# Summing the constant row b2 Wv Wo on VectorE from the PSUM blocks of Wv Wo, in place of 24 TensorE passes

## The chip, the core and the metric

The kernel runs on one core of a Trainium2 chip: TensorE (PE) with its weight loads (PEld), VectorE (DVE), ScalarE (ACT), GpSimd (POOL), and SyncE (SP), which issues most DMAs. The metric is the device time of one execution in microseconds (us), inputs and output in HBM. Lower is better.

## What is computed

Sixteen batches of 256 rows of 512 go through one cross-attention over a context of 384 columns and then a feed-forward layer with ternary weights. The part that matters here is the attention's value path:

```python
x2 = layernorm(modality2, ln2_g, ln2_b)      # (.. - mu) * rsqrt(var + EPS) * g2 + b2
v  = x2 @ Wv + bv
attn = softmax(q @ k.T * scaling)
ctx = attn @ v
return ctx @ Wo + bo
```

The rows of `attn` sum to one, so what does not depend on the row of the context leaves the softmax unchanged. With n the normalised context without gain and bias, the result is attn n diag(g2) Wv Wo plus one constant row, (b2 Wv + bv) Wo + bo. The kernel prepares the matrix diag(g2) Wv Wo (`Wvo`, three blocks of 128 rows by 512) and the constant row (`crow`, repeated over all 128 partitions) once, in its prologue.

## The kernel before

Eight groups of 512 rows (two batches, four tiles of 128 rows) are worked on. The body of group b does the feed-forward layer of b (16 steps of `up`, `sq`, `hi`, `lo`, `down`) and, between them, the attention of group b+1. All of it runs in float32, or in pairs of a high half (ScalarE writes it) and a low half (VectorE writes it by subtraction).

Before the first body there is a prologue of about 95 us. It prepares the weights and does the attention of group 0. It is written out by hand: one list of words for each engine (`PROLOGUE`, L166 on), and each engine works through its list in order. Engines meet by semaphores only. The words that matter here:

- `turn:n` (PE), `sides:n` or `tern:n` (DVE), `abs:n` and `store:n` (ACT): the 32 pieces of the ternary weights. ACT sums absolute values of a piece (L817), POOL makes scales from four sums (`scale`, L633 to L640), DVE compares (`sides`: L1093, L1094; `tern`: L1088, L1089), PE turns the piece into an O bank (L1339, L1343), ACT stores it (L837). `sides:n` and `tern:n` wait for `turn:n-4`; `turn:n` waits for `store:n-4`.
- Jobs, in the order of PE's list (`JOBS`). Job n writes bank H0 or H1, whichever n's parity says, and first waits until the bank's last reader is done with job n-2 (`job_read`). For a job that both ACT and DVE read, that is DVE's semaphore `job_dve`.
- `wvT:c`: transpose of a block of Wv, copied by ACT (L687). `wvo:c`: block c of Wv Wo, eight passes from `WvT` and `Wo_s` (L1167). ACT writes the high half scaled by g2 (L695), then DVE the low half (L892).
- `bv:0`: b2 Wv as a column, 24 passes of `Wv_s` against b2 (L1152); DVE adds bv and writes `bvp` (L882). `coacc` (DVE): the four blocks of Wo, each scaled by a column of `bvp`, summed into `bvrep` (L1034, L1036), each of the four waiting for the one before. `co:0`: PE sums `bvrep` over the partitions with a matrix of ones (L1171), DVE adds bo and writes `crow` (L897).
- `M:c`: blocks of Wq Wk^T (L1160, low half L887). `n1T:t`, `n2T:t`: transposes of the normalised input tiles (L1209); ACT makes those inputs (`nx`, L767; `nc`, L793). `fb:0` (L1176): the low-rank part. `t:0` to `t:2` (L1183): the first products of group 0's attention; they need M and all transposes.

At the prologue's end ACT normalises group 1's rows (L767), and SyncE issues their moves as small DMAs (L505), on which group 1's `t` waits in body 0.

Of the kernel before, what the change touches and what calls it, by code (L numbers as in the profile page):

```python
# [29 lines left out]
P = 128  # L30
ALU = mybir.AluOpType
# [5 lines left out]
HI, LO = 0, 1  # L37
# [109 lines left out]
def body_steps(b, engine):  # L147
# [11 lines left out]
    for j in (NFF - 3, NFF - 2):  # L159
# [62 lines left out]

JOB_KINDS = ("wqT", "wkT", "M", "bq", "wvT", "bv", "wvo", "co", "fb")
JOBS = [(word.partition(":")[0], int(word.partition(":")[2])) for word in PROLOGUE["pe"]
# [3 lines left out]
def mk_xattn_ffn(nc, x, ctx_768, ln1_g, ln1_b, ln2_g, ln2_b, Wq, bq, Wk, bk, Wv, bv, Wo, bo,  # L228
# [7 lines left out]
    NG = NB * S // TOK  # L236
# [7 lines left out]
    with ExitStack() as stack:  # L244
# [22 lines left out]
        bvc = vcols[:, 2 * KD + 2 * KC:NV]  # L267
        bvp = sb("bvp", [P, KE])
        gatec = sb("gatec", [P, 1])
# [105 lines left out]
        ident_made, identb_made, ones_made = sem("ident_made"), sem("identb_made"), sem("ones_made")  # L375
        bq_summed, co_summed = sem("b1_Wq_summed"), sem("bv_Wo_summed")
        tb_products, tb_made = sem("tbias_products"), sem("tbias_made")
# [100 lines left out]
        def _(sp):  # L478
# [79 lines left out]
            for b in range(NG - 1):  # L558
# [12 lines left out]
                if b + 2 < NG:  # L571
                    move_n1(b + 2)
            store(6, 0)
            for t in range(3):
# [271 lines left out]
        def _(dve):  # L846
# [14 lines left out]
            def job(n):  # L861
# [15 lines left out]
                elif kind == "bq":  # L877
                    dve.wait_ge(bq_in, 16)
                    nc.vector.tensor_tensor(x2a[:, KC, :], bank[:, :], bqrow, ALU.add).then_inc(job_dve, 1)
                elif kind == "bv":  # L880
                    dve.wait_ge(vcols_made, 1)
                    nc.vector.tensor_tensor(bvp[:, :], bank[:, :].rearrange("p (k n) -> p k n", k=KE)[:, :, 0], bvc[:, :],  # L882
                                            ALU.add).then_inc(job_dve, 1)
                    dve.wait_ge(job_dve, job_count(n, "dve"))
                elif kind == "M":
# [4 lines left out]
                elif kind == "wvo":  # L890
                    dve.wait_ge(job_act, job_count(n, "act"))
                    nc.vector.scalar_tensor_tensor(out=Wvo[:, LO, c, :], in0=bank[:, :], scalar=g2c[:, c:c + 1],  # L892
                                                   in1=Wvo[:, HI, c, :], op0=ALU.mult, op1=ALU.subtract
                                                   ).then_inc(job_dve, 1)
                elif kind == "co":
# [71 lines left out]
            def steps(b, todo, odd=None):  # L967
# [3 lines left out]
                for st in todo:  # L971
# [58 lines left out]
                    elif kind == "coacc":  # L1030

                        acc = bvrep[:, :, :].rearrange("p k n -> p (k n)")
                        dve.wait_ge(wo_in, 16)
                        link(nc.vector.tensor_scalar(acc, Wo_s[:, 0, :], bvp[:, 0:1], None, ALU.mult))  # L1034
                        for k in range(1, KE):
                            last = nc.vector.scalar_tensor_tensor(out=acc, in0=Wo_s[:, k, :], scalar=bvp[:, k:k + 1],  # L1036
                                                                  in1=acc, op0=ALU.mult, op1=ALU.add)
                            if k < KE - 1:
                                link(last)
                        last.then_inc(co_summed, 1)  # L1040
                    elif kind[:2] in ("xs", "cs"):
# [83 lines left out]
        def _(pe):  # L1125
            pe.wait_ge(ident_made, 1)

            def job(n):
# [14 lines left out]
                elif kind == "bq":  # L1143
# [3 lines left out]
                    mm = pe.matmul(bank[:, :], ones[:, :], x2a[:, 0, :], start=True, stop=True)  # L1147
                elif kind == "bv":
                    pe.wait_ge(vcols_made, 1)
                    for e in range(KE):  # L1150
                        for k in range(KC):
                            mm = pe.matmul(bank[:, e * P:(e + 1) * P], Wv_s[:, k, e * P:(e + 1) * P],  # L1152
                                           b2c[:, k:k + 1].broadcast_to([P, P]), start=(k == 0), stop=(k == KC - 1))
                elif kind == "M":
# [14 lines left out]
                elif kind == "co":  # L1169
                    pe.wait_ge(co_summed, 1)  # L1170
                    mm = pe.matmul(bank[:, :], ones[:, :], bvrep[:, :, :].rearrange("p k n -> p (k n)"),  # L1171
                                   start=True, stop=True)
                elif kind == "fb":
                    pe.wait_ge(lowrank_in, 16 * 7)
                    for k in range(KD):
                        mm = pe.matmul(bank[:, k * 64:(k + 1) * 64], v_s[:, k * P:(k + 1) * P],  # L1176
                                       fbT4[:, :, :].rearrange("s i r -> s (i r)"), start=True, stop=True)
# [226 lines left out]
```

## Time and profile before

| | |
|---|---|
| median of 3 runs | 805.66 us (803.67 to 807.49) |
| the profiled execution's own time | 805.04 us |
| its span in the trace | 803.0 us |
| PE busy in the span | 777.0 us (97%), 3877 matmul instructions |
| PEld busy | 642.9 us (80%) |
| DVE busy | 543.3 us (68%) |
| ACT busy | 374.9 us (47%) |
| POOL busy | 150.0 us (19%) |

The span runs from the first to the last instruction seen, and 2.04 us of the execution lie around it. The shares are means over the whole span; the change lies in some 25 us of the prologue, whose shares are others. A row of the timeline gives start and length; rows of one engine overlap a little, because the length runs to the end of writing. So what an instruction costs its engine is read from its start to the next one's.

### The profile page before, as it was taken

What the parts mean: (1) busy time and instruction counts of PE and PEld (TensorE: products, weight loads), DVE (VectorE), ACT (ScalarE), POOL (GpSimd) and SP (SyncE); (2) the same over time, 40 slices, a digit from 0 to 9 for tenths busy, and PEclk for the clock granted to TensorE, in tenths of its full rate; (3) what the DMA queues carried; (4) which work ended last, traced back from release to release, by engine and by line L of the source; (5) the groups of instructions that cost most, each with busy time, mean ns of one, the idle gap of its engine ahead of it and who ended that gap; (6) DMA issues with size and microseconds to landing.
All of it is one profiled execution on the core that took longest, in us unless ns stands there. A gap on an engine that the chain in (4) does not pass through costs nothing.

```text
span 803.0 us, 10829 instructions
## 1 busy us (share of the span) xinstructions
PE 777.0 (97%) x3877; PEld 642.9 (80%) x3877; DVE 543.3 (68%) x1100; ACT 374.9 (47%) x705; POOL 150.0 (19%) x171
## 2 busy tenths in 40 slices
PE   6999988999999999999999999999999999999998
PEld 4678767887888778887888788887888788888886
DVE  5998857667757685577766685577766686476434
ACT  5997545335551644326542554326542554424332
POOL 3241130112202022022201122012301122012001
PEclk9999999999999999999999999999999999999999
DMA  9753141034410551134410452124420441021001
GB/s 314 273 144 102 17 77 56 36 54 69 127 40 1 85 112 53 40 46 69 118 57 1 70 86 94 40 36 74 98 83 0 70 75 55 0 35 45 27 0 53
DMA packets 180554, 56.93 MB, mean 71 GB/s; under 512 B 167666, under 2 KB 168068, under 8 KB 180500
## 3 DMA queue, kind: packets, MB, share of 16 engines
q1 hardware_dynamic: 150368, 51.51, 26.2%
q10 hardware_dynamic: 30132, 4.73, 3.4%
q8 instruction: 31, 0.51, 0.3%
q14 instruction: 23, 0.19, 0.1%
HBM read 27.64 MB, written 8.39 MB: 45 GB/s over the span
## 4 chain that ended last, share of the span: by engine, by line
PE 77%; SPq 6%; DVE 5%; ACT 3%; ACTq 3%; DMA 3%; issue 2%; DVEq 0%
PE G L1183 23%; PE O L1299 22%; PE H L1318 22%; SPq L505 5%; ACTq L788 3%; PE H L1324 3%; DVE rbuf L1074 2%; DMA Wv_s<-in_L_xattn_Wv_dram 2%; ACT rbuf L749 1%; PE H L1167 1%; PE G L1265 1%; PE O L1372 1%; DMA n_blocks<-n_rows 1%; PE H L1183 1%; ACT qbuf L757 1%
## 5 line engine op out<-in xcount | busy, mean ns | idle before, releaser
L1299 PE MATMUL O<-projT,qbuf 128*128 128x512 f32 x992 | 246.9, 391 | 6.7 <-DVE qbuf L1078 6.7
L1299 PEld LDWEIGHTS O<-projT,qbuf 128*128 128x128 f32 x992 | 184.1, 188 | 47.7 <-DVE qbuf L1078 10.6
L757 ACT ACTIVATE qbuf<-rbuf 128x512 fp32r<-128x512 f32 x125 | 79.1, 633 | 148.5 <-DVE rbuf L1074 112.1
L1074 DVE TENSOR_TENSOR rbuf<-rbuf 128x512 f32<-128x512 f32 x128 | 95.5, 746 | 61.9 <-ACT rbuf L749 61.8
L1318 PE MATMUL H<-even_group,fcT 128*128 128x512 f32 x512 | 127.8, 392 | 2.9 <-ACT rbuf L749 2.9
L1318 PE MATMUL H<-odd_group,fcT 128*128 128x512 f32 x512 | 127.3, 391 | 0.0
L749 ACT ACTIVATE rbuf<-H,scf 128x512 f32<-128x512 f32 x128 | 86.9, 679 | 68.2 <-PE H L1324 63.2
L1318 PEld LDWEIGHTS H<-even_group,fcT 128*128 128x128 f32 x512 | 94.9, 188 | 22.4 <-ACT rbuf L749 3.3
L1078 DVE TENSOR_TENSOR qbuf<-rbuf,qbuf 128x512 fp32r<-128x512 f32 x125 | 88.8, 710 | 33.7 <-ACT qbuf L757 30.9
L1318 PEld LDWEIGHTS H<-odd_group,fcT 128*128 128x128 f32 x512 | 95.3, 188 | 19.3
L1183 PE MATMUL G<-Wvo,tT 128*128 128x512 f32 x270 | 65.6, 391 | 0.0
L1183 PEld LDWEIGHTS G<-Wvo,tT 128*128 128x128 f32 x270 | 50.5, 188 | 11.2 <-DVE tT L944 0.4
L1324 PE MATMUL H<-tstack,uT 128*128 128x512 f32 x128 | 49.9, 390 | 0.0
L617 POOL TENSOR_TENSOR nrs<-nrs,mhalf 128x1 f32<-128x1 f32 x32 | 25.7, 804 | 125.3 <-DVE nrs L924 125.3
L612 POOL TENSOR_TENSOR xrs<-xrs,mhalf 128x4 f32<-128x4 f32 x8 | 8.4, 1051 | 187.7 <-DVE xrs L1058 187.7
L940 DVE SCALAR_TENSOR_TENSOR tT<-G,tbias,tT 128x512 fp32r<-128x512 f32 x23 | 17.2, 748 | 30.8 <-ACT tT L730 30.8
L767 ACT ACTIVATE n_rows<-xb,xnm,xrs 128x512 f32<-128x512 f32 x28 | 22.4, 811 | 29.9 <-issue 29.9
L1183 PE MATMUL G<-odd_group,M 128*128 128x512 f32 x144 | 33.6, 390 | 2.2 <-DVE tT L940 2.2
L1183 PEld LDWEIGHTS G<-n2T,tT 128*128 128x128 f32 x261 | 33.6, 190 | 2.5 <-DVE tT L940 1.4
L1183 PE MATMUL G<-n2T,tT 128*128 128x256 f32 x261 | 35.0, 283 | 0.0
L944 DVE TENSOR_TENSOR tT<-G,tT 128x512 fp32r<-128x512 f32 x22 | 15.2, 691 | 27.6 <-ACT tT L733 27.6
L1183 PEld LDWEIGHTS G<-odd_group,M 128*128 128x128 f32 x144 | 27.0, 188 | 8.1 <-DVE tT L940 2.6
(196 smaller groups left out, 1066.9 us busy)
## 6 DMA issues: line engine op xcount, KB each, us to landing
xb<-in_x_dram SPq DMA_DIRECT2D x8, 1024.0 KB, 4.8
n_blocks<-n_rows SPq DMA_DIRECT2D x112, 64.0 KB, 2.3
ctxb<-in_ctx_dram SPq DMA_DIRECT2D x8, 768.0 KB, 4.3
n_blocks<-ctxb SPq DMA_DIRECT2D x112, 48.0 KB, 2.1
wring<-in_L_ffn_w_fc_dram SPq DMA_DIRECT2D x16, 256.0 KB, 5.3
wring<-in_L_ffn_w_proj_dram SPq DMA_DIRECT2D x16, 256.0 KB, 3.1
out_dram<-x2a SPq DMA_DIRECT2D x8, 512.0 KB, 3.0
x_blocks<-x_rows SPq DMA_DIRECT2D x56, 64.0 KB, 3.0
```

Of the source, the lines that this page charges most:

```text
L505: sp.dma_start(*block_of(blocks, rows, i, q)).then_inc(moved, 16)
L617: nc.gpsimd.tensor_tensor(nrs[:, t:t + 1], nrs[:, t:t + 1], mhalf[:, 0:1], ALU.pow).then_inc(rstd_made, 1)
L749: nc.scalar.activation(rbuf[:, j % 2, :], banks[f"H{j % 2}"][:, :], ACT.Relu, scale=scf[:, j:j + 1]).then_inc(relu_made, 1)
L757: nc.scalar.activation(squares(b, j)[:, HI, :], rbuf[:, j % 2, :], ACT.Copy).then_inc(sqhi_made, 1)
L767: nc.scalar.activation(nrm[:, t % 2, :] if g == 0 else n1_rows[:, t, :], xb[:, t, :], ACT.Identity, scale=xrs[:, t:t + 1], bias=xnm[:, t:t ...
L788: act.dma_start(*block_of(x_blocks, x_rows, i, q)).then_inc(x_moved, 16)
L1074: nc.vector.tensor_tensor(rbuf[:, j % 2, :], rbuf[:, j % 2, :], rbuf[:, j % 2, :], ALU.mult).then_inc(square_made, 1)
L1078: nc.vector.tensor_tensor(squares(b, j)[:, LO, :], rbuf[:, j % 2, :], squares(b, j)[:, HI, :], ALU.subtract).then_inc(sqlo_made, 1)
L1183: mm = pe.matmul(bank, w, m, start=(first and i == 0), stop=(last and i == len(pairs) - 1))
L1299: mm = pe.matmul(banks[f"O{t}"][:, :], qbuf[:, j % 2, h, t * P:(t + 1) * P], projT[:, j, :], start=(j == 0 and h == HI), stop=(j == NFF - ...
L1318: pe.matmul(banks[f"H{j % 2}"][:, :], fcT[:, k, j * P:(j + 1) * P], xnT[:, h, k, :], start=(k == 0 and h == HI), stop=False)
L1324: pe.matmul(banks[f"H{j % 2}"][:, :], uT[:, j * P:(j + 1) * P], tstack[:, :], start=False, stop=True).then_inc(up_full, 1)
```

## The change

The job `bv:0` goes, with its 24 passes, `bvp` and its addition. `coacc` now scales Wo's blocks by bv alone and stands ahead of `wvo:0` in DVE's list. Each `wvo:c` on DVE gets a second instruction: after the low half it adds b2's column times the block as it stands in PSUM (before the gain) to the same `bvrep`. `co:0` waits for the last of these. Since b2 Wv Wo is the sum over all rows of Wv Wo scaled by b2, and `co:0` sums over partitions, `crow` comes out the same.

```diff
     "pe": (
...
-        "n1T:1 M:2 turn:4 turn:5 bv:0 turn:6 turn:7 wvT:2 n1T:2 wvo:0 turn:8 turn:9 n1T:3 turn:10 turn:11 wvo:1 wvo:2 "
+        "n1T:1 M:2 turn:4 turn:5 turn:6 turn:7 wvT:2 n1T:2 wvo:0 turn:8 turn:9 n1T:3 turn:10 turn:11 wvo:1 wvo:2 "
...
     "dve": (
...
-        "sides:6 tern:7 cs23 n1T:0 n1T:1 M:2 bv:0 tern:8 tern:9 tern:10 sides:11 sides:12 tern:13 wvo:0 sides:14 "
-        "tern:15 coacc n1T:2 n1T:3 wvo:1 wvo:2 tern:16 sides:17 sides:18 co:0 sides:19 n2T:0 n2T:1 M:3 n2T:2 n2T:3 "
+        "sides:6 tern:7 cs23 n1T:0 n1T:1 M:2 tern:8 tern:9 tern:10 sides:11 sides:12 tern:13 coacc wvo:0 sides:14 "
+        "tern:15 n1T:2 n1T:3 wvo:1 wvo:2 tern:16 sides:17 sides:18 co:0 sides:19 n2T:0 n2T:1 M:3 n2T:2 n2T:3 "
...
-JOB_KINDS = ("wqT", "wkT", "M", "bq", "wvT", "bv", "wvo", "co", "fb")
+JOB_KINDS = ("wqT", "wkT", "M", "bq", "wvT", "wvo", "co", "fb")
...
                 elif kind == "wvo":
                     dve.wait_ge(job_act, job_count(n, "act"))
                     nc.vector.scalar_tensor_tensor(out=Wvo[:, LO, c, :], in0=bank[:, :], scalar=g2c[:, c:c + 1],
-                                                   in1=Wvo[:, HI, c, :], op0=ALU.mult, op1=ALU.subtract
-                                                   ).then_inc(job_dve, 1)
+                                                   in1=Wvo[:, HI, c, :], op0=ALU.mult, op1=ALU.subtract)
+                    acc = bvrep[:, :, :].rearrange("p k n -> p (k n)")
+                    dve.wait_ge(co_parts, KE)
+                    if c > 0:
+                        dve.wait_ge(job_dve, job_count(JOBS.index(("wvo", c - 1)), "dve"))
+                    nc.vector.scalar_tensor_tensor(out=acc, in0=bank[:, :], scalar=b2c[:, c:c + 1], in1=acc,
+                                                   op0=ALU.mult, op1=ALU.add).then_inc(job_dve, 1)
...
                         dve.wait_ge(wo_in, 16)
-                        link(nc.vector.tensor_scalar(acc, Wo_s[:, 0, :], bvp[:, 0:1], None, ALU.mult))
+                        dve.wait_ge(vcols_made, 1)
+                        nc.vector.tensor_scalar(acc, Wo_s[:, 0, :], bvc[:, 0:1], None, ALU.mult).then_inc(co_parts, 1)
                         for k in range(1, KE):
-                            last = nc.vector.scalar_tensor_tensor(out=acc, in0=Wo_s[:, k, :], scalar=bvp[:, k:k + 1],
-                                                                  in1=acc, op0=ALU.mult, op1=ALU.add)
-                            if k < KE - 1:
-                                link(last)
-                        last.then_inc(co_summed, 1)
+                            dve.wait_ge(co_parts, k)
+                            nc.vector.scalar_tensor_tensor(out=acc, in0=Wo_s[:, k, :], scalar=bvc[:, k:k + 1],
+                                                           in1=acc, op0=ALU.mult, op1=ALU.add).then_inc(co_parts, 1)
...
                 elif kind == "co":
-                    pe.wait_ge(co_summed, 1)
+                    job_read(pe, JOBS.index(("wvo", KC - 1)))
```

VectorE's instructions from block 0 of `Wvo` to its block 1 (`wvo:0`, `sides:14`, `tern:15`, `coacc`, the n1 halves, `wvo:1` and `wvo:2`) stand so before:

```order
L892 SCALAR_TENSOR_TENSOR Wvo<-H,vcols,Wvo 128x512 [waits job_act,job_full]
L1093 TENSOR_SCALAR above<-wring,half 128x512 [waits tern_turned,scales_made]
L1094 TENSOR_SCALAR below<-wring,minus_half 128x512
L1088 TENSOR_SCALAR below<-wring,minus_half 128x512 [waits tern_turned,scales_made]
L1089 SCALAR_TENSOR_TENSOR above<-wring,half,below 128x512 [waits dve_chain]
L1034 TENSOR_SCALAR bvrep<-x2a,bvp 128x512 [waits wo_in]
L1036 SCALAR_TENSOR_TENSOR bvrep<-x2a,bvp,bvrep 128x512 [waits dve_chain] x3
L934 TENSOR_TENSOR even_group<-G,even_group 128x4x128 [waits unit_act] x2
L892 SCALAR_TENSOR_TENSOR Wvo<-H,vcols,Wvo 128x512 [waits job_act,job_full] x2
```

The same place on VectorE in the changed program (its line numbers are its own; `x2a` is the buffer that holds Wo):

```order
L1034 TENSOR_SCALAR bvrep<-x2a,vcols 128x512 [waits vector_columns_made,wo_in]
L1037 SCALAR_TENSOR_TENSOR bvrep<-x2a,vcols,bvrep 128x512 [waits bv_Wo_parts_summed] x3
L886 SCALAR_TENSOR_TENSOR Wvo<-H,vcols,Wvo 128x512 [waits job_act,job_full]
L892 SCALAR_TENSOR_TENSOR bvrep<-H,vcols,bvrep 128x512 [waits bv_Wo_parts_summed]
L1091 TENSOR_SCALAR above<-wring,half 128x512 [waits tern_turned,scales_made]
L1092 TENSOR_SCALAR below<-wring,minus_half 128x512
L1086 TENSOR_SCALAR below<-wring,minus_half 128x512 [waits tern_turned,scales_made]
L1087 SCALAR_TENSOR_TENSOR above<-wring,half,below 128x512 [waits dve_chain]
L933 TENSOR_TENSOR even_group<-G,even_group 128x4x128 [waits unit_act] x2
L886 SCALAR_TENSOR_TENSOR Wvo<-H,vcols,Wvo 128x512 [waits job_act,job_full]
L892 SCALAR_TENSOR_TENSOR bvrep<-H,vcols,bvrep 128x512 [waits job_dve,bv_Wo_parts_summed]
```

The four instructions of `coacc` moved from behind `tern:15` to ahead of block 0's low half, and each block now has two instructions that read its bank (the third pair follows).

TensorE's passes for the three blocks, the ones product (`co`) and the last block of M, with the banks' numbers, before:

```order
L1167 MATMUL H1<-x2a,WvT 128x512 [waits job_act,wo_in,job_dve]
...
L1167 MATMUL H0<-x2a,WvT 128x512 [waits job_act]
...
L1167 MATMUL H1<-x2a,WvT 128x512 [waits job_act,job_dve]
...
L1171 MATMUL H0<-bvrep,ones 128x512 [waits bv_Wo_summed,job_dve]
L1160 MATMUL H1<-WkT,WqT 128x384 [waits job_act,job_dve]
```

The same in the changed program:

```order
L1159 MATMUL H0<-x2a,WvT 128x512 [waits job_act,wo_in,job_dve]
...
L1159 MATMUL H1<-x2a,WvT 128x512 [waits job_act]
...
L1159 MATMUL H0<-x2a,WvT 128x512 [waits job_act,job_dve]
...
L1163 MATMUL H1<-bvrep,ones 128x512 [waits job_dve]
L1152 MATMUL H0<-WkT,WqT 128x384 [waits job_act,job_dve]
```

With one job less the banks change places; the third block still waits for VectorE to have read the first, and the ones product now waits for VectorE's last reading of the third block.

## Rows read from the trace of the kernel before

**Rows 1.** Busy time by stretch: length, each engine busy (count), clock, DMA share.

```profile
31.00:46.00 15.00, 15.00 (x94) 9.05 (x93) 13.73 (x26) 14.56 (x35) 3.50 (x10) 1.00 0.61 170
46.00:54.00 8.00, 8.00 (x63) 6.02 (x62) 7.62 (x18) 7.95 (x22) 4.18 (x7) 1.00 0.40 134
...
124.00:803.00 679.00, 668.36 (x3194) 558.90 (x3194) 447.78 (x886) 288.39 (x512) 114.65 (x107) 1.00 0.26 55
```

**Rows 2.** The chain that ended last, prologue: start, length, what.

```profile
28.52 2.73 PE H L1152 x24
...
32.81 3.44 PE H L1167 x8
36.24 0.45 PE O L1339 x8
...
37.80 6.92 PE H L1167 x16
...
53.62 2.98 PE G L1183 x12
```

**Rows 3.** The same chain, from the prologue's end into body 0.

```profile
92.57 2.94 ACT n_rows L767 x4
95.53 0.75 SPq L505
...
123.95 3.02 PE G L1183 x12
```

**Rows 4.** Timeline of VectorE: start, length, what, idle before it and releaser.

```profile
30.25 0.61 DVE L887 SCALAR_TENSOR_TENSOR M<-H,vcols,M 128x384 fp32r<-128x384 f32 x1
31.29 0.16 DVE L882 TENSOR_TENSOR bvp<-H,vcols 128x4 f32<-128x4 f32 x1 [0.44 <-PE H L1152]
31.49 0.49 DVE L1088 TENSOR_SCALAR below<-wring,minus_half 128x512 bf16<-128x512 f32 x1
...
36.58 0.49 DVE L1093 TENSOR_SCALAR above<-wring,half 128x512 bf16<-128x512 f32 x1 [0.65 <-PE O L1339]
...
37.37 0.48 DVE L1088 TENSOR_SCALAR below<-wring,minus_half 128x512 bf16<-128x512 f32 x1
...
38.56 0.75 DVE L892 SCALAR_TENSOR_TENSOR Wvo<-H,vcols,Wvo 128x512 fp32r<-128x512 f32 x1
39.22 0.48 DVE L1093 TENSOR_SCALAR above<-wring,half 128x512 bf16<-128x512 f32 x1
...
41.20 0.48 DVE L1034 TENSOR_SCALAR bvrep<-x2a,bvp 128x512 f32<-128x512 f32 x1
41.71 2.33 DVE L1036 SCALAR_TENSOR_TENSOR bvrep<-x2a,bvp,bvrep 128x512 f32<-128x512 f32 x3
43.95 1.28 DVE L934 TENSOR_TENSOR even_group<-G,even_group 128x512 fp32r<-128x512 f32 x2
45.15 1.41 DVE L892 SCALAR_TENSOR_TENSOR Wvo<-H,vcols,Wvo 128x512 fp32r<-128x512 f32 x2
46.47 0.48 DVE L1088 TENSOR_SCALAR below<-wring,minus_half 128x512 bf16<-128x512 f32 x1
```

**Rows 5.** Timeline of GpSimd.

```profile
31.15 0.22 POOL L640 TENSOR_SCALAR minus_half<-scf 128x4 f32<-128x4 f32 x1
```

**Rows 6.** Timeline of ScalarE.

```profile
34.66 0.85 ACT L767 ACTIVATE nrm<-xb,xnm,xrs 128x512 f32<-128x512 f32 x1
35.37 1.11 ACT L837 ACTIVATE fcT<-O 128x512 fp32r<-128x512 f32 x2
...
44.76 0.69 ACT L695 ACTIVATE Wvo<-H,vcols 128x512 fp32r<-128x512 f32 x1 [0.24 <-PE H L1167]
```

**Rows 7.** Timeline of TensorE: three places.

```profile
9.38 1.97 PE L1142 MATMUL H<-ident,Wq_s 128*128 128x128 f32 x8 [3.03 <-ACT WqT L684]
...
46.24 1.08 PE L1171 MATMUL H<-bvrep,ones 128*128 128x512 f32 x2
...
89.98 0.63 PE L1209 MATMUL H<-ident,nrm 128*128 128x128 f32 x4 [1.26 <-DVE nrm L1067]
```

More of the change, by code:

```diff
@@ L267, in mk_xattn_ffn @@
         bvc = vcols[:, 2 * KD + 2 * KC:NV]
-        bvp = sb("bvp", [P, KE])
         gatec = sb("gatec", [P, 1])
@@ L375, in mk_xattn_ffn @@
         ident_made, identb_made, ones_made = sem("ident_made"), sem("identb_made"), sem("ones_made")
-        bq_summed, co_summed = sem("b1_Wq_summed"), sem("bv_Wo_summed")
+        bq_summed, co_parts = sem("b1_Wq_summed"), sem("bv_Wo_parts_summed")
         tb_products, tb_made = sem("tbias_products"), sem("tbias_made")
@@ L572, in _ @@
                     move_n1(b + 2)
-            store(6, 0)
+            store(NG - 2, 0)
             for t in range(3):
@@ L879, in job @@
                     nc.vector.tensor_tensor(x2a[:, KC, :], bank[:, :], bqrow, ALU.add).then_inc(job_dve, 1)
[L880 to L884, printed above, removed]
                 elif kind == "M":
@@ L1147, in job @@
                     mm = pe.matmul(bank[:, :], ones[:, :], x2a[:, 0, :], start=True, stop=True)
[L1148 to L1153, printed above, removed]
                 elif kind == "M":
```

## The prediction

> **What bounds the kernel now.** I read first the busy time by stretch, for the stretch that the change touches, since the shares of the whole span say nothing of it. TensorE is busy 15.00 of 15.00 us from 31 to 46 us, but VectorE is at 13.73 and ScalarE at 14.56; from 46 to 54 us it is 8.00 of 8.00 with VectorE at 7.62 and ScalarE at 7.95 [rows 1]. Three engines are full at once, so work can't be passed from one to another for free. The chain of waits comes second. It stays on TensorE through the prologue's middle: the 24 passes with b2 (2.73 us), the block 0 of Wv Wo (3.44 us), blocks 1 and 2 (6.92 us), and so on to the product `t:0` at 53.62 us [rows 2]. Seen from this chain alone, 24 passes less are 2.73 us less. The third view is the timeline of each engine around the same places; it tells who would be late once the passes are gone. Last, what a shift at `t:0` does later: the chain goes on over ScalarE's n rows at 92.57 us, the queue of SyncE that moves them from 95.53 us, and arrives at group 1's `t:0` at 123.95 us [rows 3]. Each of these waits for the one before and none for a fixed moment; in the bodies TensorE is busy 668.36 of 679.00 us [rows 1]. So a shift of `t:0` in the prologue reaches the end one to one.
>
> **The prices.** A step costs from its start to the next one's start.
> - `tern` costs 1.19 us (37.37 to 38.56) and `sides` 0.79 (36.58 to 37.37) [rows 4].
> - The low half of a block costs VectorE 0.66 us (38.56 to 39.22; two in 1.32, 45.15 to 46.47), with its data in PSUM. The new instruction has the same form, operands and size, so 0.66 as well. Bounds: nothing below 0.66, and 0.75 if it waits for its predecessor, as in `coacc`, where three took 2.24 us from 41.71 to 43.95 [rows 4]. I take 0.66: between two additions into `bvrep` stands a low half.
> - `coacc` costs 2.75 us (41.20 to 43.95), the two halves of n1T 1.20 (43.95 to 45.15) [rows 4]. It is moved, not changed: still four instructions, each waiting for the one before.
> - Removed on VectorE: `bvp` with 0.20 us (31.29 to 31.49), and 0.44 us of waiting for TensorE ahead of it [rows 4].
>
> The Trainium skill ("VectorE: DVE Perf Modes", section "The DRAIN you can't avoid") says that a semaphore after each VectorE operation costs nothing extra. The rows disagree by a little: 0.75 with such a wait and 0.66 without it. By the page `coacc` would take some 0.3 us less, and my estimate would come out near +1.3 us and not +1.6; the sum goes by the rows.
>
> **TensorE, until it must wait.** Without the passes it reaches `turn:6` 2.73 us earlier, and then meets other waits.
> 1. Block 0 (`wvo:0`) is now job 14 and needs job 12, `M:2`, read by VectorE: that row runs from 30.25 to 30.86 [rows 4]. So it starts at 30.95 at the earliest and ends at 34.4 (3.44 us), 1.8 us earlier than before.
> 2. `n1T:3` needs ScalarE's row that runs from 34.66 to 35.51, and `turn:11` needs the second of the two stores from 35.37 to 36.48 [rows 6]. ScalarE is full and doesn't wait for TensorE there, so neither comes earlier. Then 0.45 us of turning [rows 2], and block 1 starts at 37.0. Before, it started 0.7 us later. Of the 2.73 us, 2.0 are lost by here.
> 3. Block 1 ends at 40.4. Block 2 needs block 0 read by VectorE, now by both instructions.
>
> **VectorE.** `tern:8` started at 31.49, behind `bvp`. But it needs GpSimd's scales too, and the last of those ends at 31.37 [rows 5], so it starts at about 31.45: the 0.44 us of waiting stay. The wait of 0.65 us ahead of `sides:12` [rows 4] is for `turn:8`, which now ends at 34.6, and goes. From 31.45: three `tern` (35.0), two `sides` (36.6), `tern:13` (37.8), `coacc` (40.55), low half and addition of block 0, 2 x 0.66 (41.9). Before, the low half of block 0 was read at 39.3. `coacc` ahead of it, 2.75 us, is on TensorE's path now: what is queued behind it is the reading that frees block 2's bank.
>
> **The stall.** Block 2 starts on TensorE at 42.0, when it could at 40.4: a new wait of 1.5 us. It ends at 45.5, where before blocks 1 and 2 together ended at 44.7. ScalarE's high half of block 2, at 44.76 before with 0.24 us of waiting [rows 6], comes at 45.7 and ends at 46.35. VectorE, from 41.9: `sides:14` (42.7), `tern:15` (43.9), n1T (45.1), block 1's pair (46.4), block 2's pair (47.7, written at 47.85). Both routes arrive together at 46.4.
>
> **The ones product** started at 46.24 [rows 7] because TensorE was free then; its sum had been ready from about 44. It now waits for 47.85 and starts at about 47.9: **1.6 us later**. TensorE waits before it, with M's last block, the n2 transposes, `fb` and three turns queued behind. These stood without a gap from 46.24 to `t:0` at 53.6, all 8.00 us of it busy [rows 1], so they hand the 1.6 us on whole.
>
> **The sum.** TensorE: -2.73 (passes), +2.0 (waits for ScalarE's rows and stores and for M:2 ahead of block 1), +1.5 (block 2 waits for block 0's reading), +0.85 (the ones product waits for block 2's addition) = +1.6 us. VectorE counted by itself up to the end of block 2's pair: +1.98 (three additions), -0.65 (wait gone), -0.04 = +1.3; before, TensorE went on without waiting for that pair. 805.04 + 1.6 = 806.6 us for an execution like the profiled one. That lies 0.62 us under the median of the runs shown, so for a median I say 805.66 + 1.6 = 807.3 us.
>
> This is 0.2%, less than the 0.5% (4 us) that a measurement of this kernel tells from no change.
>
> **Rivals.**
> - *The passes come back as time.* Speaks for it: the 24 passes are in the chain and nothing on TensorE's own side needs them. Against: full VectorE and ScalarE, and `coacc` ahead of block 0. If VectorE could be hidden, 805.66 - 2.73 = 802.9; with block 1 at 37.0 as worked out and no wait behind it, -0.65, 805.0. Chance 0.10 for all that ends below before by 0.3 us or more.
> - *The shift is swallowed later.* The change then adds its wait, but a wait on another engine's work behind `t:0` ends last anyway: 805.7. Speaks for it that TensorE idles 1.26 us ahead of 89.98 [rows 7] and 10.64 of 679 us in the bodies [rows 1]; against, that these waits are for engines which wait for the attention of group 0 themselves. Chance 0.16.
> - *Slower by more than can be missed.* TensorE's clock has two levels, 1.2 and 2.4 GHz. At 9.38 us, after 3.03 us of idling, 8 transposes take 1.97 us, and after 1.26 us of idling at 89.98 us four take 0.63 [rows 7], though the granted clock reads 1.00 wherever I looked [rows 1]. If the new wait of 1.5 us and the one ahead of the ones product brought the lower level back, TensorE's 20 us of work from 42 to 62 us would take up to twice as long: at the worst 817. It decides from 2.4 us lost (4 less 1.6), that is 4.8 us at the lower level. The wait of 1.26 us left no trace of this, and mine is hardly longer. Chance 0.05.
> - *The stall is larger in kind*, at +2.6: the additions at 0.75 instead of 0.66 (+0.3), and ScalarE's stores and sums, late by the wait for block 2, hold back `turn` and `nc` steps in turn (0.2 to 0.7). 808.3. It belongs to the forecast's own range, which is +0.8 to +2.6, 806.5 to 808.3. The lower end is that wherein the M and transposes behind the ones product have slack that the trace doesn't show. Chance for forecast and this together 0.69.
>
> The additions have no other effect on the DMAs: `sides:14` and `tern:15` are made 2.5 us later, so two weight pieces are loaded that much later, and ScalarE needs them 6 us after their issue, when it is late by 0.9 us itself. At a landing time like the rest that just holds; if not, it is part of the +2.6.
>
> **How the numbers follow.** The mechanism's ends, 806.5 and 808.3, widened by the half spread of the runs (1.9 us), reach 804.6 to 810.2; to hold the swallowed case and part of the first rival I go down to 804.0, and I close at 809.8. Outside lie the whole gain and the clock. Faster by over 0.5%: even the full gain is 0.34%, so only the spread could do it, 0.02. Slower by over 0.5%: the clock, and the spread on top of the +2.6, 0.06. The rest, 0.92, is within.
>
> **What the trace will show.** Right, if block 0 starts on TensorE near 31.0 and block 1 near 37.0; TensorE idles about 1.5 us ahead of block 2, released by VectorE's addition; the ones product starts near 47.9, released by the third addition, and `t:0` near 55.2; ScalarE idles over 1 us before block 2's high half; VectorE has no idle time at `sides:12`, but keeps some 0.5 us ahead of `tern:8`. Group 1's `t:0` then comes near 125.5. Wrong in the first place if `coacc` is shorter or starts earlier than 37.8, or if the ones product starts before 46.3; wrong in the second if `t:0` is late and group 1's is not.

## The result

The change makes the kernel slower by a quarter of a per cent: 806.69 us against 805.20 us (medians of 22 runs each), ratio 1.0024 with a 95% interval of 1.0017 to 1.0031. That is 1.9 us (1.4 to 2.5). The ratio weighs all the runs and is not that of the two medians, which lie 1.5 us apart; the means, 807.07 and 805.20, lie 1.9 us apart. The difference is inside what was called "no change to tell" (0.5%), and resolved only because there were so many runs. The forecast was +1.6 us. The profiled execution after took 805.78 us, span 803.9 us.

TensorE's timeline of the changed kernel (start, length, what, and in brackets the idle time ahead and its releaser):

```profile
30.94 3.70 PE L1159 MATMUL H<-x2a,WvT 128*128 128x512 f32 x8 [0.29 <-DVE M L881]
...
35.66 0.63 PE L1201 MATMUL G<-ident,nrm 128*128 128x128 f32 x4 [0.57 <-ACT nrm L766]
...
37.07 3.65 PE L1159 MATMUL H<-x2a,WvT 128*128 128x512 f32 x8
41.97 3.70 PE L1159 MATMUL H<-x2a,WvT 128*128 128x512 f32 x8 [1.25 <-DVE bvrep L892]
...
48.06 1.10 PE L1163 MATMUL H<-bvrep,ones 128*128 128x512 f32 x2 [0.71 <-DVE bvrep L892]
...
53.60 1.01 PE L1201 MATMUL G<-ident,ctxb 128*128 128x128 f32 x6 [0.28 <-DVE n2T L936]
...
55.78 3.02 PE L1175 MATMUL G<-even_group,M 128*128 128x512 f32 x12
```

The same timeline before, for blocks 1 and 2 and for `t:0`:

```profile
37.64 7.08 PE L1167 MATMUL H<-x2a,WvT 128*128 128x512 f32 x16
...
53.59 3.02 PE L1183 MATMUL G<-even_group,M 128*128 128x512 f32 x12
```

The changed kernel has five new waits. Before, TensorE had none between 31 and 54 us [rows 1]. Block 0 starts 1.7 us earlier than before and waits for VectorE's low half of M; `n1T:3` waits for ScalarE's rows; block 2 waits 1.25 us for VectorE's addition of block 0; the ones product waits 0.71 us for the addition of block 2, and starts at 48.06 instead of 46.24 [rows 7]; the n2 transposes wait 0.28 us for VectorE's n2 low halves. `t:0` starts at 55.78; before, at 53.59.

The idle time in brackets is shorter than what a wait costs, since a row's length reaches past the start of what follows it. Counted from start to start, a block takes 3.46 us (16 passes in the 6.92 us of [rows 2]), so the wait ahead of block 2 costs 41.97 - 37.07 - 3.46 = 1.44 us.

VectorE's timeline of the changed kernel shows who releases them:

```profile
31.43 0.49 DVE L1086 TENSOR_SCALAR below<-wring,minus_half 128x512 bf16<-128x512 f32 x1 [0.54 <-POOL minus_half L639]
...
37.76 0.48 DVE L1034 TENSOR_SCALAR bvrep<-x2a,vcols 128x512 f32<-128x512 f32 x1
38.27 2.33 DVE L1037 SCALAR_TENSOR_TENSOR bvrep<-x2a,vcols,bvrep 128x512 f32<-128x512 f32 x3
40.52 0.74 DVE L886 SCALAR_TENSOR_TENSOR Wvo<-H,vcols,Wvo 128x512 fp32r<-128x512 f32 x1
41.18 0.74 DVE L892 SCALAR_TENSOR_TENSOR bvrep<-H,vcols,bvrep 128x512 f32<-128x512 f32 x1
...
46.50 0.75 DVE L886 SCALAR_TENSOR_TENSOR Wvo<-H,vcols,Wvo 128x512 fp32r<-128x512 f32 x1
47.17 0.74 DVE L892 SCALAR_TENSOR_TENSOR bvrep<-H,vcols,bvrep 128x512 f32<-128x512 f32 x1
...
50.59 0.69 DVE L896 TENSOR_TENSOR crow<-H,borow 128x512 f32<-128x512 f32 x1
51.19 0.48 DVE L1091 TENSOR_SCALAR above<-wring,half 128x512 bf16<-128x512 f32 x1
51.58 1.50 DVE L1092 TENSOR_SCALAR below<-wring,minus_half 128x512 bf16<-128x512 f32 x1
```

`coacc` stands from 37.76 to 40.52, and block 0's bank is free at 41.9, where before it was read by 39.3 [rows 4]. The last row is one that nobody asked for: a comparison of `sides:19` that takes 1.50 us and not 0.48. GpSimd's timeline beside it:

```profile
51.41 2.79 POOL L654 TENSOR_TENSOR x2a<-xb,crow 128x512 f32<-128x512 f32 x2 [0.20 <-DVE crow L896]
```

And ScalarE's high half of block 2, which had 0.24 us of idle time ahead of it before [rows 6]:

```profile
45.71 0.69 ACT L694 ACTIVATE Wvo<-H,vcols 128x512 fp32r<-128x512 f32 x1 [1.51 <-PE H L1159]
```

The busy time by stretch, to hold against [rows 1]: TensorE 1.92 us less in the first stretch and 0.99 less in the second, VectorE fuller in both.

```profile
31.00:46.00 15.00, 13.08 (x57) 6.45 (x58) 14.29 (x26) 13.49 (x33) 3.30 (x10) 1.00 0.61 169
46.00:54.00 8.00, 7.01 (x50) 4.92 (x47) 7.87 (x15) 6.98 (x17) 3.79 (x7) 1.00 0.29 101
```

And the chain of waits into body 0, beside [rows 3]: 1.87, 1.86 and 1.84 us later.

```profile
94.44 2.93 ACT n_rows L766 x4
97.39 0.75 SPq L504
...
125.79 3.01 PE G L1175 x12
```

**Why the span is only 0.9 us longer in this one execution.** The bodies of these two executions differ by as much as the effect. VectorE's `tstack` (L931, after L930) marks the start of each body. Here are bodies 2 and 3, of the kernel before:

```profile
282.09 0.69 DVE L931 TENSOR_TENSOR tstack<-G,tstack 64x512 fp32r<-64x512 f32 x1 [1.47 <-ACT tstack L718]
373.93 0.69 DVE L931 TENSOR_TENSOR tstack<-G,tstack 64x512 fp32r<-64x512 f32 x1 [1.46 <-ACT tstack L718]
```

and of the changed one:

```profile
283.69 0.69 DVE L930 TENSOR_TENSOR tstack<-G,tstack 64x512 fp32r<-64x512 f32 x1 [1.45 <-ACT tstack L717]
374.00 0.69 DVE L930 TENSOR_TENSOR tstack<-G,tstack 64x512 fp32r<-64x512 f32 x1 [1.49 <-ACT tstack L717]
```

Body 2 takes 91.84 us in the one and 90.31 in the other, with the same instructions; body 5 goes the other way (90.60 us before, 91.44 after). Over all eleven profiles of this study each of the bodies 2 to 5 falls near 90.4 or near 91.6 us, in the kernel before too. So the experiments are read at two places of their own trace as well, both ahead of this: the start of `t:0`, and group 0's `tstack`. Both are counted from the low half of M:2 on VectorE (30.25 us before, 30.28 after, up to 31.02 in others), since the first loads arrive at slightly different times in each execution. Each kernel has one trace, so a number of the table is one execution's. How far such a number can be trusted is seen at one place: from the ones product to `t:0` the kernel before and six others (e1, e2, e4, f1, f3, g1) all take 7.35 to 7.37 us.

### The profile page after: what moved, and what is told of

The parts are those of the page before. It is cut to its first block, busy times and chain, and to the rows that moved or that the text cites. A ratio compares the mean times of both kernels' runs of the same rounds, so it can differ in the third digit from the quotient of the medians.

```text
span 803.9 us, 10784 instructions
## 1 busy us (share of the span) xinstructions
PE 776.1 (97%) x3853; PEld 641.0 (80%) x3853; DVE 544.7 (68%) x1102; ACT 374.3 (47%) x705; POOL 149.9 (19%) x171
## 4 chain that ended last, share of the span: by engine, by line
PE 75%; DVE 7%; SPq 6%; ACT 4%; issue 3%; ACTq 2%; DMA 2%; DVEq 0%
PE G L1175 23%; PE O L1291 22%; PE H L1310 22%; SPq L504 5%; PE H L1316 3%; ACTq L787 2%; DVE rbuf L1072 2%; ACT rbuf L748 1%; PE G L1257 1%; PE O L1364 1%; DMA crow<-in_L_xattn_bq_dram 1%; DMA n_blocks<-n_rows 1%; PE H L1175 1%; DVE below L1092 1%; PE H L1152 1%
## 5 line engine op out<-in xcount | busy, mean ns | idle before, releaser
L1072 DVE TENSOR_TENSOR rbuf<-rbuf 128x512 f32<-128x512 f32 x128 | 93.2, 728 | 61.1 <-ACT rbuf L748 60.9
```

Source lines behind the costliest of these rows:

```text
L1072: nc.vector.tensor_tensor(rbuf[:, j % 2, :], rbuf[:, j % 2, :], rbuf[:, j % 2, :], ALU.mult).then_inc(square_made, 1)
```

## The experiments

All times in us. "Against before" is the difference to the kernel before.

| kernel | t:0 from M:2 | against before | tstack from M:2 | against before | ratio of times, 95% interval |
|---|---|---|---|---|---|
| before | 23.34 | | 65.77 | | |
| changed | 25.50 | +2.16 | 67.59 | +1.82 | 1.0024 [1.0017, 1.0031] |
| e1_move_only | 24.33 | +0.99 | 66.72 | +0.95 | 1.0009 [0.9999, 1.0018] |
| e2_no_additions | 23.60 | +0.26 | 65.69 | -0.08 | 0.9995 [0.9986, 1.0004] |
| e3_bank_early | 25.98 | +2.64 | 68.07 | +2.30 | 1.0039 [1.0027, 1.0052] |
| e4_residual_late | 25.15 | +1.81 | 67.75 | +1.98 | 1.0029 [1.0017, 1.0042] |
| f1_narrow | 24.79 | +1.45 | 67.17 | +1.40 | 1.0013 [1.0003, 1.0023] |
| f2_meet | 24.06 | +0.72 | 66.43 | +0.66 | 1.0012 [1.0002, 1.0021] |
| f3_passes_gone | 22.75 | -0.59 | 64.84 | -0.93 | 0.9984 [0.9975, 0.9993] |
| g1_sides_first | 25.15 | +1.81 | 67.23 | +1.46 | 1.0021 [1.0012, 1.0030] |
| g2_co_behind_m | 25.03 | +1.69 | 67.11 | +1.34 | 1.0017 [1.0007, 1.0027] |

### What the passes are worth by themselves

`f3_passes_gone`, from the kernel before:

```diff
-        "n1T:1 M:2 turn:4 turn:5 bv:0 turn:6 turn:7 ...
+        "n1T:1 M:2 turn:4 turn:5 turn:6 turn:7 ...
-        "sides:6 tern:7 cs23 n1T:0 n1T:1 M:2 bv:0 tern:8 ...
+        "sides:6 tern:7 cs23 n1T:0 n1T:1 M:2 tern:8 ...
```

> The kernel before with the 24 passes and their job taken out and nothing in their place; coacc stands where it stood. The constant row lacks b2 Wv Wo. This is the most that removing the passes can bring in this order of work. Theory S: block 1 on TensorE at 37.0, block 2 at 40.5 without a wait, but ScalarE stays full, its nc:3 and high halves come at most 0.3 to 0.5 us earlier, and t:0 starts at 53.0 to 53.3 (before 53.59), not 2.73 us earlier; ratio 0.999 to 1.000. Rival G (the passes are worth what they take): t:0 at 50.9 to 51.5, ratio 0.997.

TensorE's timeline:

```profile
36.40 0.63 PE L1196 MATMUL G<-ident,nrm 128*128 128x128 f32 x4 [0.58 <-ACT nrm L766]
37.82 7.08 PE L1154 MATMUL H<-x2a,WvT 128*128 128x512 f32 x16
...
53.77 3.03 PE L1170 MATMUL G<-even_group,M 128*128 128x512 f32 x12
```

This execution began 0.77 us late (M:2 at 31.02), so `t:0` is 0.59 us earlier than before, counted from M:2; by the timed runs the kernel is 1.3 us faster (0.6 to 2.0), a little more than theory S had in its ratio. Taking 2.73 us of work out of the chain that ends last, and putting nothing in its place, brings 0.6 of them at `t:0`, and at most 2.0 by the timed runs. TensorE waits for ScalarE's rows, which wait for nothing: in this trace ScalarE has no wait of 0.1 us or more from 31 to 56 us. Rival G is out.

### The place of coacc

`e1_move_only`, from the kernel before:

```diff
-        "... sides:12 tern:13 wvo:0 sides:14 tern:15 coacc n1T:2 ...
+        "... sides:12 tern:13 coacc wvo:0 sides:14 tern:15 n1T:2 ...
```

> The kernel before with one part of the change: the four instructions of coacc stand ahead of block 0's low half on VectorE; the 24 passes and their job stay, and there are no additions from PSUM. Theory S (what counts is when VectorE gets to each reading): the low half of block 0 ends near 42.0 us and not 39.3, block 2 on TensorE starts near 42.05 (before 41.1), the ones product near 47.2 (before 46.24), t:0 near 54.5 (before 53.59, changed kernel 55.78); about +0.9 us in all, ratio 1.001. Rival N (the place of coacc costs nothing, the additions alone do): t:0 at 53.6 to 53.7, ratio 1.000.

TensorE's timeline:

```profile
42.19 3.70 PE L1167 MATMUL H<-x2a,WvT 128*128 128x512 f32 x8 [0.83 <-DVE Wvo L892]
...
54.75 3.01 PE L1183 MATMUL G<-even_group,M 128*128 128x512 f32 x12
```

No instruction was added or removed, and `t:0` is 0.99 us later: the wait ahead of block 2 (0.83 us of idle time; 42.19 against 37.71 + 3.46 from start to start, 1.02 us) is for the reading of block 0 behind `coacc`. Theory S held, rival N is out. This rests on the trace; the timed runs alone don't tell +0.9 us from nothing (1.0009, 0.9999 to 1.0018).

### Both, and then the additions

`e2_no_additions`, from the changed kernel:

```diff
                     nc.vector.scalar_tensor_tensor(out=Wvo[:, LO, c, :], in0=bank[:, :], scalar=g2c[:, c:c + 1],
-                                                   in1=Wvo[:, HI, c, :], op0=ALU.mult, op1=ALU.subtract)
-                    ...
-                    nc.vector.scalar_tensor_tensor(out=acc, in0=bank[:, :], scalar=b2c[:, c:c + 1], in1=acc,
-                                                   op0=ALU.mult, op1=ALU.add).then_inc(job_dve, 1)
+                                                   in1=Wvo[:, HI, c, :], op0=ALU.mult, op1=ALU.subtract
+                                                   ).then_inc(job_dve, 1)
...
-                    job_read(pe, JOBS.index(("wvo", KC - 1)))
+                    pe.wait_ge(co_parts, KE)
```

> The changed kernel without the three additions from PSUM: the constant row lacks b2 Wv Wo. The 24 passes are gone, coacc stands ahead of block 0. Theory S: block 1 on TensorE at 37.0, block 2 at 41.3 (waits for block 0's low half, 41.2), the ones product no longer waits for VectorE and starts near 46.3, t:0 near 53.7: the whole gain of the passes is lost to waits even so, ratio 1.000. Then the additions cost 2.1 us of the 2.2. Rival N (the place costs nothing, only additions do): block 2 near 40.5, t:0 near 52.9, ratio 0.999.

TensorE's timeline, block 2:

```profile
41.51 3.70 PE L1154 MATMUL H<-x2a,WvT 128*128 128x512 f32 x8 [0.59 <-DVE Wvo L886]
```

Block 2 still waits for the reading of block 0, as theory S had it, and the ones product waits for nothing; rival N is out. `t:0` +0.26 (the sum of the two above would be +0.40), the time within noise. So what the passes gave, the place of `coacc` takes, and the step from here to the changed kernel, 1.90 us at `t:0`, is the additions.

`e3_bank_early` gives the bank of block 0 back early and leaves VectorE's load nearly as it is, from the changed kernel (the four blocks of Wo are now all added to a sum that stands already, so the first of them, a product before, is an addition too):

```diff
-        "... tern:13 coacc wvo:0 sides:14 tern:15 n1T:2 ...
+        "... tern:13 wvo:0 sides:14 tern:15 coacc n1T:2 ...
...
+                    if c == 0:
+                        nc.vector.tensor_scalar(acc, bank[:, :], b2c[:, 0:1], None, ALU.mult).then_inc(job_dve, 1)
```

> The changed kernel with the same sum in another order: block 0's low half comes first, b2 times block 0 starts the sum, and the four blocks of Wo are added behind tern:15 as in the kernel before. The work of VectorE is the same or 0.1 to 0.3 us more; only the bank of block 0 is free about 2.5 us earlier. Theory S (VectorE's load up to the third addition sets the ones product): block 2 starts near 40.5 without a wait, but the ones product is still at 48.1 to 48.5 (changed kernel 48.06) and t:0 at 55.6 to 56.2 (changed kernel 55.78); ratio 1.002 to 1.003. Rival B (the wait for the bank of block 0 is what costs): the ones product near 46.8, t:0 near 54.4, ratio 1.001 or less.

TensorE's timeline:

```profile
37.07 7.09 PE L1162 MATMUL H<-x2a,WvT 128*128 128x512 f32 x16
...
48.52 1.10 PE L1166 MATMUL H<-bvrep,ones 128*128 128x512 f32 x2 [1.96 <-DVE bvrep L894]
```

VectorE's four additions of Wo:

```profile
41.44 3.11 DVE L1040 SCALAR_TENSOR_TENSOR bvrep<-x2a,vcols,bvrep 128x512 f32<-128x512 f32 x4
```

Blocks 1 and 2 run without a wait, and the ones product is later still: 0.47 us later than in the changed kernel, `t:0` 0.48 us. Theory S held in kind, but all three of its numbers came out past the upper end (48.52, 56.25, and the ratio of five runs, 1.0039). VectorE has more to do here: the four instructions take 3.02 us from start to start and not 2.76, and it idles 0.30 us for ScalarE ahead of block 0's low half. The wait for the bank was no cost of its own; it was part of the way to the third addition, and as soon as it goes the rest appears ahead of the ones product. Rival B is out: VectorE's work up to the third addition sets that time.

`g2_co_behind_m` takes the wait ahead of the ones product away as well, by order alone, from the changed kernel:

```diff
-        "... turn:15 co:0 M:3 n2T:1 turn:16 fb:0 n2T:2 n2T:3 turn:17 turn:18 turn:19 t:0 "
+        "... turn:15 M:3 n2T:1 turn:16 co:0 n2T:2 n2T:3 turn:17 turn:18 turn:19 fb:0 t:0 "
```

> The changed kernel with the ones product (co) behind M:3 and n2T:1 in TensorE's list, fb behind the turns, sides:19 ahead of the n2 low halves, and the other engines' lists to match; the work is the same. Theory S (the third addition costs because the ones product stands first in TensorE's queue behind it): M:3 starts near 47.3, the ones product near 50.4 without a wait, and t:0, from the low half of M:2, 24.3 to 24.7 us later (changed kernel 25.50, before 23.34), now set by VectorE's load; ratio to before 1.001. It stays slower than before, since the additions are still VectorE's. Rival V (VectorE's load alone sets t:0, TensorE's wait was idle time that cost nothing): t:0 at 25.1 to 25.5.

TensorE's timeline:

```profile
50.13 1.08 PE L1163 MATMUL H<-bvrep,ones 128*128 128x512 f32 x2
51.75 1.01 PE L1201 MATMUL G<-ident,ctxb 128*128 128x128 f32 x6 [0.54 <-DVE n2T L936]
```

The ones product no longer waits, M:3 fills its place, and a wait of 0.54 us for VectorE's n2 low half stands behind it. `t:0` comes 25.03 us behind M:2's low half: 0.12 us earlier than `g1_sides_first` (below), which has `sides:19` at nearly the same place and still that wait. That is just outside what either theory gave, and near rival V. My claim that TensorE's order there costs something like a microsecond fell. What is left is VectorE's load, whichever wait shows it; that is concluded from e3 and g2 together, since no run here takes other load off VectorE and keeps the three additions.

### The comparison that took 1.50 us

`e4_residual_late` (changed kernel) and `f2_meet` (kernel before) move GpSimd's additions, the one away from `sides:19`, the other onto it; `g1_sides_first` (changed kernel) moves `sides:19` away:

```diff
 e4: -scale:5 residual:0 residual:1 scale:6     +scale:5 scale:6 residual:0 residual:1
 f2: -scale:4 scale:5 residual:0 residual:1     +scale:4 residual:0 residual:1 scale:5
 g1: -sides:18 co:0 sides:19 n2T:0              +sides:18 sides:19 co:0 n2T:0
```

> The changed kernel with GpSimd's first two residual tiles behind its scale:6, so that they no longer start at 51.4 us, right behind the constant row. Theory P: in the changed kernel one comparison of VectorE (from 51.58 us) took 1.50 us and not 0.48, because it met GpSimd's addition from 51.41 on; without that addition it takes 0.48 again, the n2 low halves follow 1.0 us earlier, and t:0 comes at 55.0 to 55.3 and not 55.78; ratio to before 1.0015 to 1.002. Rival: the long comparison was an accident of that execution and has nothing to do with GpSimd: t:0 at 55.1 here too, but then other kernels in which the residual meets the same comparison (the third one of this call) don't show a long one either.

> The kernel before with GpSimd's scale:5 behind the first two residual tiles, so that the first of these starts right when the constant row is written (49.9 us, before 50.74) and meets the comparisons of sides:19 (49.83 and 50.23 us on VectorE). Theory P (a comparison of VectorE that meets GpSimd's addition waits for it): one of the two takes 1.2 to 1.5 us and not 0.48, the n2 low halves start 0.7 to 1.0 us later (50.62 before), t:0 0.4 to 0.9 us later (53.59 before), ratio 1.0005 to 1.001. Rival (the long comparison in the changed kernel came from something else): all comparisons 0.48, t:0 at 53.6.

> The changed kernel with VectorE's sides:19 ahead of its co:0, so that behind the constant row only operations follow that read PSUM. Theory P (only the comparison suffers from GpSimd's addition): no long comparison near 52 us, the n2 low halves take their 0.5 us each although GpSimd adds beside them; measured from the low half of M:2 (30.28 in the changed kernel), t:0 starts 25.1 to 25.3 us later (changed kernel 25.50, before 23.34) and group 0's tstack 67.2 to 67.4 (changed 67.59, before 65.77); ratio to before 1.0015 to 1.002. If instead the meeting costs whatever stands there: t:0 at 25.5 again.

`f2_meet`, VectorE and GpSimd at the same time; before, this comparison took 0.48 us:

```profile
49.92 1.49 DVE L1094 TENSOR_SCALAR below<-wring,minus_half 128x512 bf16<-128x512 f32 x1
49.74 2.79 POOL L655 TENSOR_TENSOR x2a<-xb,crow 128x512 f32<-128x512 f32 x2 [5.45 <-DVE crow L897]
```

`e4_residual_late`: nothing long near 52 us, but further on

```profile
65.11 1.30 DVE L1091 TENSOR_SCALAR above<-wring,half 128x512 bf16<-128x512 f32 x1
61.10 5.02 POOL L654 TENSOR_TENSOR x2a<-xb,crow 128x512 f32<-128x512 f32 x4
```

`g1_sides_first`: the n2 low halves, which read PSUM and one operand in SBUF, beside the same addition

```profile
52.55 1.19 DVE L936 TENSOR_TENSOR n2T<-G,n2T 128x384 fp32r<-128x384 f32 x2
52.77 2.50 POOL L654 TENSOR_TENSOR x2a<-xb,crow 128x512 f32<-128x512 f32 x2 [0.67 <-DVE crow L896]
```

Theory P held in all three. A comparison that starts just behind GpSimd's addition takes 1.0 us more, wherever the meeting is made. One that runs already when the addition starts is not held: in the changed kernel the one at 51.19 takes its 0.48 us, and the two additions of GpSimd take 2.79 us and not the 2.50 of `g1`. The low halves are not held: their pair takes 1.19 us beside the addition in `g1` and 1.20 in `e4`, where GpSimd adds nothing beside them. The meeting costs 0.35 us at `t:0` in the changed kernel (25.50 against 25.15 in both others). In `e4` the gain is given back at 65.11 (tstack 67.75, and the timed ratio, 1.0029, is above the 1.0015 to 1.002 expected), in `g1` it is kept (67.23). By time alone the changed kernel, `e4` and `g1` can't be told apart. The rival, an accident of one execution, is out: the same 1.50 stands in `e3_bank_early` at 52.05.

`g2_co_behind_m` has such a meeting too, with an addition of VectorE's whose two operands both lie in SBUF; in the kernel before it takes 0.42 us:

```profile
55.14 1.47 DVE L1103 TENSOR_TENSOR u_s<-u_s,urs 128x256 f32<-128x256 f32 x1
53.81 2.51 POOL L654 TENSOR_TENSOR x2a<-xb,crow 128x512 f32<-128x512 f32 x2 [2.34 <-DVE crow L896]
```

It starts behind g2's `t:0` (55.06), so it doesn't touch the number above.

### Passes over one column

`f1_narrow`, from the kernel before:

```diff
-                            mm = pe.matmul(bank[:, e * P:(e + 1) * P], Wv_s[:, k, e * P:(e + 1) * P],
-                                           b2c[:, k:k + 1].broadcast_to([P, P]), ...
+                            mm = pe.matmul(bank[:, e * P:e * P + 1], Wv_s[:, k, e * P:(e + 1) * P],
+                                           b2c[:, k:k + 1], ...
```

> The kernel before with its 24 passes kept, each over one column of b2 and not over 128 equal ones (only one column of the result was ever read). Nothing else changes. Theory S (the 2.73 us of the passes are mostly covered by others' work): the passes take 1.0 to 2.0 us and not 2.73; TensorE then waits for ScalarE's n rows ahead of n1T:3 (35.5 us), block 1 starts at 37.0 to 37.3 and not 37.64, t:0 at 52.9 to 53.4 and not 53.59, ratio 0.999 to 1.000. Rival G (what TensorE saves comes back whole): t:0 earlier by the whole saving, 51.9 to 52.6, ratio 0.998.

TensorE's timeline and the busy time by stretch (the last three numbers are granted clock, DMA share and GB/s):

```profile
28.09 2.79 PE L1152 MATMUL H<-vcols,Wv_s 128*128 128x1 f32 x24
30.75 0.22 PE L1339 MATMUL O<-identb,above 128*128 128x128 bf16 x1
...
31.88 1.06 PE L1142 MATMUL H<-ident,Wv_s 128*128 128x128 f32 x4
...
31.00:32.00 1.00, 1.00 (x12) 1.00 (x10) 0.74 (x3) 1.00 (x4) 0.21 (x2) 0.50 0.04 14
```

Both theories missed. The passes take 2.66 us, as before, with 1/128 of the columns: 0.111 us each. And from 31 to 34 us the granted clock is 0.50, the lower level (1.00 there in all ten other traces); the transposes of `wvT:2` take 1.06 us and not 0.61. By block 1 this execution is 1.45 us late, and `t:0` is late by the same. What one column is worth can't be told from this kernel.

## Why the prediction was right

**Step by step.** The early part fell as worked out: block 0 at 30.94 (forecast 30.95), block 1 at 37.07 (37.0), with 2.1 of the 2.73 us lost to ScalarE's rows and stores by there (forecast 2.0); f3 shows that this is so without anything else of the change (block 1 comes 6.80 us behind M:2's low half, in the changed kernel 6.79, before 7.39). `tern:8` started at 31.43, released by GpSimd (forecast 31.45). `sides:12` had no idle time. `coacc` began at 37.76; an earlier start than 37.8 was my sign of being wrong, and this one lies within the rounding. Block 0's bank was free at 41.9 (41.9), block 2 started at 41.97 (42.0); the wait ahead of it cost 1.44 us from start to start (1.5). ScalarE idled 1.51 us ahead of block 2's high half (over 1).

**The ones product** started at 48.06 (47.9), 1.8 us later than before where 1.6 was forecast. The low half of block 2 started at 46.50 and not 46.4: ScalarE's high half was written at 46.40 (46.35), and VectorE began 0.1 us behind it. The terms of the sum, from start to start, are -2.73, +2.13, +1.44 and +0.95, together +1.79; forecast were -2.73, +2.0, +1.5 and +0.85.

**"They hand the 1.6 us on whole"** was the step that was incomplete. `t:0` is 2.16 us later counted from M:2, 0.37 more than the ones product. The chain from the ones product to `t:0` does hand on whole where nothing meets GpSimd (7.35 us before, 7.37 in e4 and g1); in the changed kernel it takes 7.72. The constant row also releases GpSimd's residual additions, and I had asked of GpSimd only what VectorE waits for, not what it would start. Before, GpSimd was still at its scales when the row was written at 49.92. It began its additions at 50.74, behind both comparisons of `sides:19` and beside low halves that it doesn't hold:

```profile
50.23 0.48 DVE L1094 TENSOR_SCALAR below<-wring,minus_half 128x512 bf16<-128x512 f32 x1
50.62 1.02 DVE L937 TENSOR_TENSOR n2T<-G,n2T 128x384 fp32r<-128x384 f32 x2
50.74 2.51 POOL L655 TENSOR_TENSOR x2a<-xb,crow 128x512 f32<-128x512 f32 x2
```

Now it is free first and begins beside `sides:19`. e4 and g1 put 0.35 us on this.

**"A shift of `t:0` reaches the end one to one"** held for 1.82 of the 2.16 us. By `tstack` of group 0 the shift is 1.82 us; 0.23 of the difference is an idle time of VectorE at 76.65 in the trace of before that the changed one lacks. The rest was not followed; in every other kernel of the table but e4 the shift at `tstack` is the smaller one too, by 0.04 to 0.35 us. So two things that I had not foreseen, +0.37 ahead of `t:0` and -0.34 behind it, cancel almost exactly, and that much of the closeness of the forecast is luck.

**What each part of the change is worth.** By `t:0`: passes -0.59 (f3), place of `coacc` +0.99 (e1), with both together +0.26 (e2) and not +0.40; the additions +1.90, of which 0.35 are the meeting with GpSimd. So 1.55 us for three instructions of 0.66, 1.98 in all. The 0.66 was right (41.18 to 41.84, 47.17 to 47.83). That less than 1.98 arrives is because without the additions TensorE doesn't wait for VectorE ahead of the ones product (e2): the first 0.4 us of them fall into time that VectorE has (in e2 it idles 0.75 us ahead of block 2's low half).

**The rivals.** That the 2.73 us of the passes come back whole is out even where nothing replaces them (f3). The swallowing later is out: 1.84 us arrive at group 1's `t:0`. The clock did not fall in the new waits: the granted clock is 1.00 in both stretches above. (The worst case that I gave for it was summed wrongly: 20 us of work at half the clock add 20 us, 827 and not 817. Nothing else hangs on it.) The sum by the semaphore rule of the Trainium skill's "VectorE: DVE Perf Modes" (section "The DRAIN you can't avoid") would have given +1.3 us; `coacc` took 2.76 us, its chained instructions 0.75 each, as the rows had it.

**The time.** 807.3 was forecast from a median of 805.66, of three runs; the medians of 22 are 0.5 us lower before (805.20), and 806.69 after. The forecast was about the difference: +1.6 against +1.9 (1.4 to 2.5).

No version that computes the whole constant row beat the kernel before. f3 bounds what any replacement of the passes could win in this order of work: 0.6 to 0.9 us by the traces, 1.3 us (0.6 to 2.0) by the timed runs. ScalarE waits for nothing then. The three additions on VectorE cost 1.9 us by the traces, more than that. A cheaper way to the same row, or another order of ScalarE's work, was not tried.

## What to carry to other kernels

Work that stands in the chain of waits is worth only the distance to the next wait: look at each engine's timeline over the same stretch for who would be late next, ahead of counting what is removed. Where three engines are full together, moving an instruction from one to another can cost most of its length there (1.55 of 1.98 us here) and give back little of it where it was (0.6 of 2.73). A wait that is removed by reordering alone can come back as another one, as it did in e3 and g2. Ask of each result that comes at a new time not only who waits for it, but what it starts, and beside what that will run.

## What was not expected of the hardware

- A comparison on VectorE (`tensor_scalar`, float32 in SBUF, 0.48 us) takes 1.49 to 1.50 us if GpSimd's float32 addition began 0.17 to 0.18 us ahead of it (three kernels), 1.30 in another. An addition of VectorE's with both operands in SBUF took 1.47 us and not 0.42 (g2). Low halves with PSUM and one SBUF operand, beside the same addition, were not held. The Trainium skill says so in "SBUF — State Buffer", section "Who interferes with whom": `tensor_scalar` in a two-port mode and GpSimd exclude one another for a whole instruction, and whoever issues first goes first. The runs agree, though no row says in which mode the comparison ran; had I weighed it against the moved constant row, the 0.35 us could have been forecast.
- A float32 pass over one column takes 0.111 us, hardly less than one over 128 (2.73 us for 24, 0.114 each). The Trainium skill's "TensorE: Matmul & The Clock Gate", section "LDWEIGHTS (loading the stationary operand)", puts the loading of 128 columns of weights at P/1.2 ns, 0.107 us by that estimate; the row agrees.
- In f1's trace the lower clock came without any idle time of TensorE, behind 24 one-column passes (0.50 from 31 to 34 us, TensorE busy in every microsecond from 28 us on). That the narrow passes brought it is likely, since no other trace has it there, but it is one trace. The lower clock also comes in body 0, after TensorE has idled 2.8 us: in nine of the eleven traces (idle times of 2.82 to 2.85 us), the changed kernel's among them, but not in the kernel before (2.87 us) nor in g1 (2.80 us). So the length of the idle time alone doesn't decide it. The row of the changed kernel; before, the same eight took 2.11 us:

```profile
111.92 3.50 PE L1310 MATMUL H<-even_group,fcT 128*128 128x512 f32 x8 [2.84 <-ACT rbuf L748]
```

  No cost of it is seen: from the start of body 0 to that of body 1 it is 95.2 us in the changed kernel and 95.5 us before.
- Bodies of the same kernel take about 90.4 or about 91.6 us, and which body takes which differs between traces. What decides it was not tried.
